# Products that nobody reads, issued in TensorE's waits ahead of the loop over batches

## The chip, the cores and the metric

The kernel runs on one core of a Trainium2 chip. The metric is the device time of one execution in microseconds (us); of several executions the median counts.

## The reference, cut to what matters

The input x has 8 batches of 512 rows of 128 numbers, fp32. One layer of attention with 16 heads of 8 numbers, then a layer norm, then a mixture of 16 experts (8 chosen for each row) and one shared net, then a layer norm.

```python
result = embeddings @ w_qkv                      # [8, 512, 384], split into q, k, v, 16 heads of 8
scores = jnp.einsum('bnqd,bnkd->bnqk', q, k) / jnp.sqrt(jnp.float32(h))
probs = jax.nn.softmax(scores, axis=-1)
ctx = jnp.einsum('bnqk,bnkd->bnqd', probs, v)
x = _layernorm(x + out)                          # out: ctx with its heads side by side
x = _layernorm(x + ffn(x))                       # ffn: the experts and the shared net
```

## The kernel before, in words

Each engine runs its own program in order; semaphores join them. PE is TensorE, DVE is VectorE, ACT is ScalarE, POOL is GpSimd, SP starts most DMAs. First all eight batches go through attention, then all eight through the nets. The 16 heads are 4 groups of 4, the 512 rows 4 tiles of 128: a unit is one group of one batch, with 16 score products (4 heads by 4 tiles).

Scores are made twice. A product of `score_q` (L832, 32 rows of the array, 512 columns, fp32r, a type whose product is one pass) has the queries on the partitions; DVE takes the maximum of each row out of PSUM (`take_maximum`, L776). PE turns a unit's 64 maxima per partition (`turn_maxima`, L882), ACT copies them, DVE or POOL splits them into two parts, and SP writes them to DRAM and loads them into two rows of `q_aug`. Then `score_k` (L839) makes the same scores with the keys on the partitions and the maxima already subtracted, ACT takes the exponential (L733), and `weigh_values` (L852, fp32, several passes) sums the values.

Order on PE: `score_q` runs two units (AHEAD = 2, 32 products) ahead of `score_k`. So there is a **prelude** before the body of batch 0: projections of batch 0 (`project_qk` L886 twice, `project_v` L891), then the wait for the first slot of `q_aug` and `k_aug` to come back from DRAM, then 32 products of `score_q`, with the turning of the first unit's maxima after the 19th. A product of `score_q` waits until DVE is done with the product that had its PSUM bank before; four banks go round. In the body, step i (0 to 63) issues `score_k(i)` and the `score_q` of two units on; after steps 5 and 8 come the projections of the next batch, after steps 11, 14, 20 and so on a `weigh_values`.

In the prelude DVE sets `k_aug` to -1 and `q_aug` to 0 in slot 0 (L811, L812) and reports it on `pads_set`; SP writes these rows to DRAM. ACT stages and rounds the projections (`first_qk`, L715, L716) into `qk_high`, DVE makes `qk_low` (L787), SP writes both to `q_rows` and `k_rows` (L519) and then loads the slots (L508, L511). The PSUM tiles `ps_k1` and `ps_k2` are unused until the body.

Of the kernel before, what the change touches and what calls it, by code (L numbers as in the profile page):

```python
# [28 lines left out]
P = 128  # L29
BATCHES, SEQ, HIDDEN = 8, 512, 128  # L30
# [98 lines left out]
def slot_user_before(i):  # L129

    j = i - 1
    while SCORE_SLOT[j % SCORES] != SCORE_SLOT[i]:
        j -= 1
    return j


def q_head_tile(i):

    return (i + 2) % GROUP, i // GROUP % TILES


def slot_loads(times):

    return DMA * 2 * times
# [285 lines left out]
def attention(nc, r, c, stream, nets_high, nets_low, nets_down, ident, x_tiles, xT, w_qkv,  # L430
              w_nets, w_downs, gate_wT, expert_bias, q_rows, k_rows, shift_rows):
    with ExitStack() as ctx:
        def sb(name, shape, dt=F32):
            return ctx.enter_context(nc.sbuf_tensor(name, shape, dt))

        def psum(name, shape):
            return ctx.enter_context(nc.psum_tensor(name, shape, F32))

        def sem(name):
            return ctx.enter_context(nc.semaphore(name))  # L440


        q_aug = sb("q_aug", [P, GROUPS, SEQ], F32R)
        k_aug = sb("k_aug", [P, GROUPS, SEQ], F32R)
# [3 lines left out]
        w_sb = sb("w_sb", [P, 3 * HIDDEN])  # L448
        qk_raw = sb("qk_raw", [P, 2, SEQ])
        qk_high = sb("qk_high", [P, 2, SEQ], F32R)  # L450
# [9 lines left out]
        ps_k = [psum(f"ps_k{i}", [P, SEQ]) for i in range(3)]  # L460
        ps_ctx = psum("ps_ctx", [P, SEQ])

        def bank(*use):
            return ps_bank[BANK[use]]
# [5 lines left out]
        pads_set = sem("pads_set")  # L470
# [355 lines left out]
        def _(pe):  # L826
            def score_q(i):

                g = i // UNIT
                h, t = q_head_tile(i)  # L830
                rows = slice(h * ROWS, (h + 1) * ROWS)
                return pe.matmul(bank("q", (i - UNIT * AHEAD) % SCORES)[:], q_aug[rows, g, t * P:(t + 1) * P],  # L832
                                 k_aug[rows, g, :], start=True, stop=True).then_inc(scores_q, 1)

            def score_k(i):

                g, t, h = i // UNIT, i // 4 % 4, i % 4
                rows = slice(h * ROWS, (h + 1) * ROWS)
                return pe.matmul(ps_k[SCORE_SLOT[i]][:], k_aug[rows, g, t * P:(t + 1) * P], q_aug[rows, g, :],  # L839
                                 start=True, stop=True).then_inc(scores_k, 1)  # L840
# [15 lines left out]
            def wait_bank(use, b, first=False, last=False, ahead=False):  # L856

                user = bank_user_before(use, first, last, ahead)
                if user is None:
                    return  # L860
                (what, n), ago = user
                b = b - ago
                if what == "q":
                    pe.wait_ge(scores_q_used, SCORES * b + n + UNIT * AHEAD + 1)
                if what == "max":
                    pe.wait_ge(shift_staged, GROUPS * b + n + 2)
                if what == "context":
                    pe.wait_ge(c.ready, 2 * b + n)
                if what == "qk":
                    pe.wait_ge(qk_staged, 2 * (b + 1) + n + 1)  # L870
                if what == "v":
                    pe.wait_ge(v_staged, b + 2)
                if what == "x1":
                    pe.wait_ge(r.x1T_ready, 1)
                if what == "gate":
                    pe.wait_ge(r.decayed, 1)
                if what == "combine":
                    pe.wait_ge(r.combine_copied, 1)

            def turn_maxima(u, parity, dst):  # L880
                pe.wait_ge(scores_q_used, UNIT * (u + 1))
                pe.transpose(dst[0:GROUP * TILES, 0:P], maxima[:, parity, :], ident[:]  # L882
                             ).then_inc(maxima_turned, 1)
# [5 lines left out]
            def project_v(dst):  # L889
                for t in range(TILES):  # L890
                    last = pe.matmul(dst[:, t * P:(t + 1) * P], xT_sb[:, t * P:(t + 1) * P],  # L891
                                     w_sb[:, 2 * HIDDEN:3 * HIDDEN], start=True, stop=True)
                last.then_inc(v_projected, 1)

            def body(b, first=False, last=False):
                for g in range(GROUPS):
                    u = GROUPS * b + g
                    maxima_of_next = not last or g < AHEAD
                    g_next = (g + AHEAD) % GROUPS
                    for i in range(UNIT * g, UNIT * (g + 1)):  # L900
                        if i == UNIT * g:

                            pe.wait_ge(shift_loaded, GROUP * DMA * (u + 1))
                        before = slot_user_before(i)
                        if not first or before >= 0:
                            pe.wait_ge(exp_done, SCORES * b + before + 1)
                        score_k(i)
                        if maxima_of_next:
                            if i == UNIT * g:

                                pe.wait_ge(slot_loaded[g_next], slot_loads(b + 1 + (g + AHEAD) // GROUPS))

                            wait_bank(("q", i), b, first, last)
                            score_q((i + UNIT * AHEAD) % SCORES)
                        if i in QK_AFTER and not last:
                            part = QK_AFTER.index(i)
                            wait_bank(("qk", part), b, first, last)
                            pe.wait_ge(xT_loaded, DMA * (b + 2))
                            project_qk(part, bank("qk", part))
                        if i == V_AFTER and not last:  # L920
                            wait_bank(("v", 0), b, first, last)
                            project_v(bank("v", 0))
                        if i == X1_AFTER and last:
                            wait_bank(("x1", 0), b, first, last)
                            turn_x1(pe, r, ident, bank("x1", 0), 0)
                        if i == CONTEXT_AFTER[0] and not first:
                            wait_bank(("context", 0), b, first, last)
                            turn_context(pe, c, ident, 2 * b - 1, 1, bank("context", 0))
                        if i == CONTEXT_AFTER[1]:
                            wait_bank(("context", 1), b, first, last)  # L930
                            turn_context(pe, c, ident, 2 * b, 0, bank("context", 1))
                        if i == GATE_AFTER and last:
                            wait_bank(("gate", 0), b, first, last)
                            pe.wait_ge(r.consts_loaded, 2 * DMA)
                            gate(pe, r, bank("gate", 0), 0)
                        if i == COMBINE_AFTER and last:
                            wait_bank(("combine", 0), b, first, last)
                            turn_combine(pe, r, ident, bank("combine", 0), 0)
                        if i + SCORES == WEIGH_AFTER[-1] and not first:
                            weigh_values(GROUPS * b - 1, GROUPS - 1, TILES - 1, None)  # L940
                        if i in WEIGH_AFTER:
                            of, t = divmod(WEIGH_AFTER.index(i), TILES)
                            weigh_values(GROUPS * b + of, of, t, None if first and of < PAIR else 2 * b + of // PAIR)
                        if i == MAX_AFTER[g] and not (last and g == GROUPS - 1):
                            wait_bank(("max", g), b, first, last)
                            turn_maxima(u + 1, (g + 1) % 2, bank("max", g))

            pe.wait_ge(xT_loaded, DMA)
            pe.wait_ge(w_loaded, DMA)

            project_qk(0, c.ps_turned)
            project_qk(1, ps_ctx)
            project_v(ps_k[0])
            for u in range(AHEAD):
                pe.wait_ge(slot_loaded[u], slot_loads(1))
                for i in range(UNIT * u, UNIT * (u + 1)):
                    wait_bank(("q", i + UNIT * AHEAD), -1, ahead=True)
                    score_q(i)
                    if i == UNIT + 2:
                        wait_bank(("max", GROUPS - 1), -1, ahead=True)  # L960
                        pe.wait_ge(ident_set, 1)
                        turn_maxima(0, 0, bank("max", GROUPS - 1))
            body(0, first=True)
            with pe.Fori(1, BATCHES - 1) as b:
                body(b)
# [313 lines left out]
```

## Time and profile before

| | |
|---|---|
| median of 3 runs | 733.43 us |
| lowest, highest | 732.75, 737.33 us |
| the profiled execution, its own time | 730.02 us |
| its span, first to last instruction | 728.3 us |
| PE busy in the span | 696.1 us (96%) |
| mean granted clock of TensorE | 0.957 |

The profiled execution took 1.7 us outside its span and was 3.4 us under the median. A granted clock of 1.00 is TensorE's 2.4 GHz, 0.50 is 1.2 GHz. A busy time of PE is modelled from the starts of pipelined products, so the step from one start to the next tells more than the duration of one.

### The profile page before, as it was taken

The page shows a single profiled execution, that of the slowest core. Times are in us where ns is not written, and L with a number is a line of the kernel's source. Part 1 is how long each engine was busy: PE and PEld are TensorE (multiplying, and loading weights), DVE is VectorE, ACT ScalarE, POOL GpSimd, SP SyncE. Part 2 cuts the span into 40 slices and gives each one's busy share as a digit, 9 for nine tenths or more (in the row PEclk, how much of TensorE's full clock was granted, in tenths as well). Part 3 has the DMA queues.
Part 4 walks back from the last instruction along what each step waited for, and adds up shares of the span by engine and source line. Part 5 has one row for each costly group of instructions (what it writes and reads, how often), then busy time and mean ns, then how long its engine had stood idle before and what let it go on. Part 6 is the DMA issues. An engine that isn't in the chain of part 4 may idle for free. (4 is left out here: it accounts for less than half of the span.)

```text
span 728.3 us, 13274 instructions
## 1 busy us (share of the span) xinstructions
PE 696.1 (96%) x3488; PEld 365.0 (50%) x3488; DVE 515.4 (71%) x1085; ACT 415.5 (57%) x779; POOL 321.3 (44%) x371
## 2 busy tenths in 40 slices
PE   2899999999999999999998999999999999999995
PEld 1333333433433343343333767666676767676663
DVE  1879999999999999999851645647555655656343
ACT  2058887988879788887776423333342434324321
POOL 3033342425225242432320665666574656565563
PEclk8559999999999999999897999999999999999998
DMA  6832241423324142241104113050605032140601
GB/s 186 240 119 78 84 155 49 153 68 91 118 81 136 51 139 80 71 154 40 38 5 186 47 73 162 17 230 0 247 0 220 26 127 119 37 209 3 244 1 29
DMA packets 34279, 74.89 MB, mean 103 GB/s; under 512 B 4144, under 2 KB 13488, under 8 KB 30032
## 3 DMA queue, kind: packets, MB, share of 16 engines
q1 hardware_dynamic: 33440, 72.38, 28.7%
q0 software_dynamic: 816, 2.23, 1.1%
q8 instruction: 11, 0.18, 0.1%
q14 instruction: 12, 0.10, 0.0%
HBM read 58.61 MB, written 15.99 MB: 102 GB/s over the span
## 5 line engine op out<-in xcount | busy, mean ns | idle before, releaser
L733 ACT ACTIVATE probs<-ps_k 128x512 f32<-128x512 f32 x512 | 268.2, 606 | 59.4 <-PE ps_k L839 56.1
L776 DVE TENSOR_REDUCE maxima<-ps_bank 128x1 f32<-128x512 f32 x384 | 245.4, 684 | 27.0 <-PE ps_bank L832 21.2
L1061 POOL TENSOR_TENSOR hidden<-gated,weights 128x512 f32<-128x512 f32 x128 | 167.1, 1312 | 124.1 <-DVE gated L1143 108.3
L1091 ACT ACTIVATE silu<-ps_gate 128x512 f32<-128x512 f32 x136 | 81.3, 598 | 176.9 <-PE ps_gate L1185 176.6
L839 PE MATMUL ps_k<-q_aug,k_aug 32*128 32x512 f32 x512 | 161.4, 498 | 3.9 <-ACT probs L733 3.7
L1143 DVE TENSOR_TENSOR gated<-silu,ps_up 128x512 f32<-128x512 f32 x128 | 87.0, 686 | 105.2 <-PE ps_up L1185 69.7
L832 PE MATMUL ps_bank<-k_aug,q_aug 32*128 32x512 f32 x384 | 149.8, 515 | 12.1 <-DMA q_aug<-q_rows 8.2
L852 PE MATMUL ps_ctx<-probs,v_ones 128*32 128x512 f32 x1024 | 142.4, 629 | 0.7 <-ACT probs L733 0.7
L1210 PE MATMUL ps_y<-hidden,nets_down 128*128 128x512 f32 x272 | 137.1, 591 | 0.0
L839 PEld LDWEIGHTS ps_k<-q_aug,k_aug 32*128 32x128 f32 x512 | 66.8, 188 | 131.9 <-ACT probs L733 111.4
L1182 PE MATMUL ps_gate<-x1T_high,nets_low 128*128 128x512 f32 x136 | 96.5, 710 | 0.0
L608 POOL TENSOR_TENSOR shift<-shift_raw,ones 16x128 fp32r<-16x128 f32 x31 | 13.8, 445 | 181.9 <-ACT shift_raw L701 181.9
L776 DVE TENSOR_REDUCE maxima<-ps_turned 128x1 f32<-128x512 f32 x128 | 87.4, 683 | 4.6 <-PE ps_bank L832 3.5
L832 PEld LDWEIGHTS ps_bank<-k_aug,q_aug 32*128 32x128 f32 x384 | 61.7, 192 | 28.1 <-DVE maxima L776 15.8
L832 PE MATMUL ps_turned<-k_aug,q_aug 32*128 32x512 f32 x128 | 65.6, 513 | 1.3
L1210 PEld LDWEIGHTS ps_y<-hidden,nets_down 128*128 128x128 f32 x272 | 51.3, 189 | 15.6 <-issue 3.8
L1185 PE MATMUL ps_gate<-x1T_low,nets_high 128*128 128x512 f32 x136 | 53.6, 394 | 0.0
L1185 PE MATMUL ps_gate<-x1T_high,nets_high 128*128 128x512 f32 x136 | 53.6, 394 | 0.0
L1185 PE MATMUL ps_up<-x1T_low,nets_high 128*128 128x512 f32 x136 | 53.4, 393 | 0.0
L1182 PE MATMUL ps_up<-x1T_high,nets_low 128*128 128x512 f32 x136 | 53.2, 391 | 0.0
L1185 PE MATMUL ps_up<-x1T_high,nets_high 128*128 128x512 f32 x136 | 53.2, 391 | 0.0
L1185 PEld LDWEIGHTS ps_gate<-x1T_high,nets_high 128*128 128x128 f32 x136 | 25.8, 190 | 24.9 <-issue 24.5
(109 smaller groups left out, 631.5 us busy)
## 6 DMA issues: line engine op xcount, KB each, us to landing
weights<-combine_rows SPq DMA_DIRECT2D x32, 1024.0 KB, 7.5
k_aug<-k_rows SPq DMA_DIRECT2D x32, 256.0 KB, 2.6
q_aug<-q_rows SPq DMA_DIRECT2D x32, 256.0 KB, 2.9
q_rows<-qk_high SPq DMA_DIRECT2D x16, 256.0 KB, 2.9
k_rows<-qk_high SPq DMA_DIRECT2D x16, 256.0 KB, 3.6
net_raw<-w_nets POOLq DMA_DIRECT2D x17, 128.0 KB, 2.4
xT_sb<-xT SPq DMA_DIRECT2D x8, 256.0 KB, 2.9
q_rows<-qk_low SPq DMA_DIRECT2D x8, 256.0 KB, 3.1
```

What stands on the lines that cost most here:

```text
L608: pool.tensor_tensor(shift[:, 0, :], shift_raw[:], r.ones[0:GROUP * TILES, 0:P], ALU.mult).then_inc(shift_high, 1)
L733: act.activation(probs[:, t, h, :], ps_k[SCORE_SLOT[i]][:], ACT.Exp, scale=ATT_SCALE).then_inc(exp_done, 1)
L776: dve.tensor_reduce(maxima[:, parity, TILES * h + t:TILES * h + t + 1], bank("q", (i - UNIT * AHEAD) % SCORES)[:], AX_X, ALU.max).then_inc ...
L832: return pe.matmul(bank("q", (i - UNIT * AHEAD) % SCORES)[:], q_aug[rows, g, t * P:(t + 1) * P], k_aug[rows, g, :], start=True, stop=True) ...
L839: return pe.matmul(ps_k[SCORE_SLOT[i]][:], k_aug[rows, g, t * P:(t + 1) * P], q_aug[rows, g, :], start=True, stop=True).then_inc(scores_k, 1)
L852: last = pe.matmul(ps_ctx[32 * h:32 * (h + 1), :], v_ones[:, g, t, h, :], probs[:, t, h, :], start=opens, stop=closes)
L1061: pool.tensor_tensor(hidden[:, s % RING, :], gated[:, s % UP_RING, :], r.weights[:, e, :], ALU.mult).then_inc(hidden_done, 1)
L1091: act.activation(silu[:, s % UP_RING, :], ps_gate[s % 2][:], ACT.Silu).then_inc(silu_done, 1)
L1143: dve.tensor_tensor(dst, silu[:, s % UP_RING, :], ps_up[s % UP_RING][:], ALU.mult).then_inc(gated_done, 1)
L1182: pe.matmul(dst[:], nets_low[:, s, j, :], r.x1T_high[:], start=True, stop=False)
L1185: return pe.matmul(dst[:], nets_high[:, s, j, :], x[:], start=False, stop=stop)
L1210: pe.matmul(ps_y[:], nets_down[:, n, :], hidden[:, n % RING, :], start=n == 0, stop=n == LAST).then_inc(down_done, 1)
```

## The change

It adds products on PE whose results go to `ps_k1` and `ps_k2` and are read by nobody, in four places: 7 products of the constants in slot 0, once DVE has set them and before the wait for the inputs; 9 products of the weights `w_sb` (fp32, 384 columns) between `project_v` and the first `score_q`; one product of `qk_high` (fp32r, 512 columns, all 128 rows) behind each of the 32 products of `score_q`; and 4 of these before the body. One wait is new, for `pads_set`. No other engine's program changes.

```diff
+            def busy_with_pads(dst):
+                pe.matmul(dst[:], k_aug[:, 0, 0:P], q_aug[:, 0, :], start=True, stop=True)
+            def busy_with_weights(dst):
+                pe.matmul(dst[:, 0:3 * HIDDEN], w_sb[:, 0:HIDDEN], w_sb[:], start=True, stop=True)
+            def busy_with_rows(dst):
+                pe.matmul(dst[:], qk_high[:, 0, 0:P], qk_high[:, 1, :], start=True, stop=True)
+            pe.wait_ge(pads_set, 2)
+            for n in range(7):
+                busy_with_pads(ps_k[1 + n % 2])
             pe.wait_ge(xT_loaded, DMA)
             pe.wait_ge(w_loaded, DMA)
             project_qk(0, c.ps_turned)
             project_qk(1, ps_ctx)
             project_v(ps_k[0])
+            for n in range(9):
+                busy_with_weights(ps_k[1 + n % 2])
             for u in range(AHEAD):
                 pe.wait_ge(slot_loaded[u], slot_loads(1))
                 for i in range(UNIT * u, UNIT * (u + 1)):
                     wait_bank(("q", i + UNIT * AHEAD), -1, ahead=True)
                     score_q(i)
+                    busy_with_rows(ps_k[1 + i % 2])
                     if i == UNIT + 2:
                         wait_bank(("max", GROUPS - 1), -1, ahead=True)
                         pe.wait_ge(ident_set, 1)
                         turn_maxima(0, 0, bank("max", GROUPS - 1))
+            for n in range(4):
+                busy_with_rows(ps_k[1 + n % 2])
             body(0, first=True)
```

On PE, from its first instruction to the first scores, before and after (L951, L954 and L957 are the three new helpers in the order of the diff):

```order
 L825 UNCONDITIONAL_BRANCH [waits barrier_Pool_Activation_PE_DVE_SP_release]
+L951 MATMUL ps_k<-q_aug,k_aug 128x512 [waits pads_set]
+L951 MATMUL ps_k<-q_aug,k_aug 128x512 x6
 L886 MATMUL ps_turned<-xT_sb,w_sb 128x512 [waits w_loaded,xT_loaded]
 L886 MATMUL ps_ctx<-xT_sb,w_sb 128x512
 L891 MATMUL ps_k<-w_sb,xT_sb 128x128 x4
+L954 MATMUL ps_k<-w_sb 128x384 x9
 L832 MATMUL ps_bank<-k_aug,q_aug 128x512 [waits slot_loaded0]
+L957 MATMUL ps_k<-qk_high 128x512
 L832 MATMUL ps_turned<-k_aug,q_aug 128x512
+L957 MATMUL ps_k<-qk_high 128x512
 L832 MATMUL ps_bank<-k_aug,q_aug 128x512
```

Nothing is moved; the projections now stand behind seven products and the first score behind nine more.

On PE, around the turning of the first unit's maxima (L882), as it stands now:

```order
L832 MATMUL ps_turned<-k_aug,q_aug 128x512 [waits scores_q_used]
L957 MATMUL ps_k<-qk_high 128x512
L882 MATMUL ps_bank<-ident,maxima 16x128 [waits scores_q_used,ident_set]
L832 MATMUL ps_bank<-k_aug,q_aug 128x512 [waits scores_q_used]
L957 MATMUL ps_k<-qk_high 128x512
L832 MATMUL ps_bank<-k_aug,q_aug 128x512 [waits scores_q_used]
L957 MATMUL ps_k<-qk_high 128x512
```

Each score there has a product of all 128 rows behind it that waits for nothing but PE.

## Rows read from the trace of the kernel before

**Rows 1.** The page: TensorE's granted clock in 40 slices of the span.
```profile
PEclk8559999999999999999897999999999999999998
```

**Rows 2.** Busy time in stretches: start:end, length, busy time of each engine (instructions), granted clock, DMA.
```profile
4.57:10.03 5.46, 5.45 (x12) 3.09 (x12) 1.26 (x2) 2.15 (x4) 0.00 (x0) 1.00 0.37 110
10.03:14.10 4.07, 0.00 (x0) 0.00 (x0) 0.12 (x1) 0.58 (x1) 2.36 (x5) 1.00 0.95 307
...
18.23:37.87 19.64, 16.54 (x34) 7.46 (x34) 17.17 (x30) 0.41 (x2) 0.00 (x0) 0.50 0.86 247
37.87:49.07 11.20, 11.20 (x32) 4.26 (x31) 8.08 (x14) 6.62 (x13) 3.81 (x5) 0.50 0.11 31
...
51.70:84.60 32.90, 32.07 (x229) 11.82 (x223) 31.17 (x54) 27.79 (x56) 10.74 (x19) 1.00 0.30 93
```

**Rows 3.** The timeline of all engines, 1 to 18.3 us: start, duration, instruction.
```profile
1.60 0.48 DVE L812 MEMSET q_aug<- 128x512 f32 x1
...
4.57 2.04 PE L886 MATMUL ps_turned<-xT_sb,w_sb 128*128 128x512 f32 x2 [4.57 <-DMA w_sb<-w_qkv]
...
7.75 1.16 SPq L519 DMA_DIRECT2D q_rows<-qk_high  x2
...
18.23 0.79 PE L832 MATMUL ps_bank<-k_aug,q_aug 32*128 32x512 f32 x1 [8.21 <-DMA q_aug<-q_rows]
```

**Rows 4.** The timeline of PE, from the first unit's turned maxima to step 12 of the body.
```profile
29.50 0.38 PE L882 MATMUL ps_bank<-ident,maxima 128*16 128x128 f32 x1
31.29 1.39 PE L832 MATMUL ps_bank<-k_aug,q_aug 32*128 32x512 f32 x2 [1.42 <-DVE maxima L776]
...
37.87 0.79 PE L839 MATMUL ps_k<-q_aug,k_aug 32*128 32x512 f32 x1
...
42.76 2.08 PE L886 MATMUL ps_turned<-xT_sb,w_sb 128*128 128x512 f32 x2
...
45.91 2.07 PE L886 MATMUL ps_turned<-xT_sb,w_sb 128*128 128x512 f32 x2
...
49.07 1.94 PE L852 MATMUL ps_ctx<-probs,v_ones 128*32 128x512 f32 x8
50.93 0.79 PE L839 MATMUL ps_k<-q_aug,k_aug 32*128 32x512 f32 x1
```

**Rows 5.** The timeline of DVE, the same stretch.
```profile
30.36 0.28 DVE L782 TENSOR_TENSOR shift<-shift_raw,shift 16x128 fp32r<-16x128 f32 x1 [1.63 <-ACT shift L706]
30.57 1.27 DVE L776 TENSOR_REDUCE maxima<-ps_bank 128x1 f32<-128x512 f32 x2
31.76 0.67 DVE L776 TENSOR_REDUCE maxima<-ps_turned 128x1 f32<-128x512 f32 x1
...
40.12 3.65 DVE L776 TENSOR_REDUCE maxima<-ps_bank 128x1 f32<-128x512 f32 x6
45.63 1.89 DVE L776 TENSOR_REDUCE maxima<-ps_bank 128x1 f32<-128x512 f32 x3 [1.85 <-PE ps_bank L832]
48.78 1.89 DVE L776 TENSOR_REDUCE maxima<-ps_bank 128x1 f32<-128x512 f32 x3 [1.27 <-PE ps_bank L832]
51.80 0.69 DVE L776 TENSOR_REDUCE maxima<-ps_turned 128x1 f32<-128x512 f32 x1 [1.13 <-PE ps_bank L832]
```

**Rows 6.** The timeline of PE at the full clock: batch 1, then the nets.
```profile
89.42 0.50 PE L839 MATMUL ps_k<-q_aug,k_aug 32*128 32x512 f32 x1
...
91.48 0.50 PE L839 MATMUL ps_k<-q_aug,k_aug 32*128 32x512 f32 x1
...
92.36 1.06 PE L852 MATMUL ps_ctx<-probs,v_ones 128*32 128x512 f32 x8
93.36 0.50 PE L839 MATMUL ps_k<-q_aug,k_aug 32*128 32x512 f32 x1
...
399.34 0.40 PE L1185 MATMUL ps_up<-x1T_high,nets_high 128*128 128x512 f32 x1
399.57 0.39 PE L1185 MATMUL ps_gate<-x1T_low,nets_high 128*128 128x512 f32 x1
```

## The prediction

> **What bounds the kernel now.** The page's slices and the busy times come first. PE is busy 96% of the span and its clock stands at 1.00 over most of it, at half only at the start and around two short places [rows 1]. So the body of attention and the nets are TensorE's, and time won or lost ahead of the body is carried to the end nearly whole. The prelude is another matter. The stretches [rows 2] show what binds it: nothing runs on PE from 10.03 to 18.23 us, while the rows of batch 0 go to DRAM and come back; from 18.23 to 37.87 DVE is busy 17.17 of 19.64 us and PE merely follows it; then to 49.07 PE is busy all of the time, at the low clock. The timelines of PE and DVE [rows 4, 5] show the order in detail.
>
> The low clock costs something in that last part alone. DVE takes a maximum every 0.60 us (30.57 to 31.76 for two) [rows 5]; a score at either clock is shorter than that, so the 19.64 us owe the clock nothing but a tenth here and there. In steps 5 to 12 of the body DVE stands still three times for PE: 1.85, 1.27 and 1.13 us, 4.25 us in all [rows 5]. Three steps with a projection take 3.15 us there (42.76 to 45.91, and 45.91 to 49.07) [rows 4], 2.06 at the full clock in batch 1 (89.42 to 91.48) [rows 6]. From 51.70 on the clock reads 1.00 [rows 2]. So **4.25 us is about all there is to win** in the body, if the clock were full from its first step.
>
> One row misleads: 4.57 to 10.03 reads 1.00, but two projections there start 1.83 us apart, as the 2.04 of the first at the start and the 2.08 of the same product at 0.50 say too [rows 3, 4]. These ran at 1.2 GHz. The clock rose only with or after them, and 4 us after the last product it was at half again, since the next row reads 0.50 [rows 2].
>
> **The prices.** At the full clock a one-pass product of 512 columns starts 0.23 us after the one before (399.34, 399.57) [rows 6]. At the low one no row of the trace has it alone on all rows of the array. `weigh_values` steps 1.86 us (49.07 to 50.93) [rows 4] against 1.00 (92.36 to 93.36) [rows 6], so the low price is 0.23 x 1.86 = 0.43, between 0.40 (if only what is streamed slows down from an overlapped start) and 0.46 (twice). An fp32 product of 512 columns steps 1.83 at the low clock; of 384 columns that is 1.37, and 0.74 at the full one by the same ratio (0.65 if the steps of the nets' fp32 products held).
>
> **Part by part.**
>
> 1. The seven products of constants start when DVE has set `q_aug`, 1.60 + 0.48 = 2.08 us [rows 3], and take 7 x 0.43 = 3.0: to 5.1. The inputs are there at 4.57. The first projection is late by 0.5 us, and with it the chain of copies and DMAs that ends at 18.23 [rows 3]. I see no cover: SP's first write of rows at 7.75 [rows 3] stands behind that projection's copy, and all later ones behind it on the same queue. If the clock has risen in the middle of the first projection, the 0.5 comes back; bounds 0 and 0.6. I take 0.5: the load lands at 18.7.
>
> 2. Now PE is dense from 2.1 us. Before, some 5.5 us of products preceded the rise; the same here puts it near 7.6, in the second projection. The rest of the projections' 5.46 us then runs at double speed, to about 9.1. Nine products of weights at 0.65 to 0.74 take 5.9 to 6.7: they end at 15.0 to 15.8. **PE then idles for 3 to 3.7 us**, to 18.7. That is the step on which the case turns. Before, the clock fell within the 4.07 us behind the last product [rows 2]. I take it that it falls here as well, some time before or just after the first scores, since the few products of 32 rows that come first are thin.
>
> 3. At the low clock a score and the product behind it cost PE 0.43 + 0.43 = 0.86 us, since the second needs all rows of the array and so neither runs beside the other. DVE wants a score every 0.60. PE becomes the bound of the prelude. The 19 scores up to the turning of the maxima take 19 x 0.86 = 16.3: from 18.7 to 35.0, where L882 stood at 29.50 [rows 4]: +5.5. From there DVE's split and its next maximum come 1.07 later and PE's next score 1.79 later (29.50, 30.57, 31.29) [rows 4, 5], as before: 36.8. Thirteen more pairs, 11.2: 48.0. Four more products, 1.7: 49.7. The body started at 37.87 [rows 4], so it is **late by 11.8 us**. The maxima's way over DRAM is covered now (turned at 35.0, needed at 49.7).
>
> 4. Something is given back in the body. DVE was four maxima behind at its start and PE had to wait for banks: steps 0 to 5 took 4.89 us (37.87 to 42.76) [rows 4]. Now DVE has caught up; the six scores behind a projection took 1.1 us there (45.91 + 2.07 to 49.07) [rows 4], so PE needs 2.2 and a turning of 0.4, and DVE, which has four banks in hand, 3.6 for six maxima. Between the two I take 3.2, which gives 1.7 back. Steps 6 to 11 give back 2 x (3.15 - 2.06) = 2.2 and the step of `weigh_values` 0.86 more, if the clock is full by then, nothing if not. The five products ahead of the body, the projections and scores behind them leave that open.
>
> The sum: 11.8 - 1.7 = +10.1 with the clock still low, +7.0 with it full from step 6. I take the middle, **+8.5**. Behind it the batches are PE's at the full clock, and nothing takes it away again. The profiled execution's 730.0 becomes 738.5; that one was 3.4 under the median, so the median is **741.9**.
>
> **The step that a rule speaks to.** From 37.87 to 49.07 PE is busy 11.20 of 11.20 us and the clock stays at 0.50 [rows 2]; these are mostly products of 32 rows with two dense projections among them. The Trainium skill ("TensorE: Matmul & The Clock Gate", Part 1) says that the default is the throttled clock and that sustained matmul activity releases it. Read as "a busy PE", the rule contradicts this row; and it would free the clock early in the 28 us of back-to-back pairs of step 3. By it the sum would be that of rival B. I weigh the row higher, because a pair there is half a thin product, but a pair is denser than what the row has, so B keeps a good chance.
>
> **Rivals.**
>
> A, the forecast: the clock falls in the wait for the slots and stays low through the pairs. Chance 0.50.
>
> B: it falls but comes back after some 6 us of pairs, as at the start. Seven pairs late by 0.26 each are 1.8; the idle 1.42 us of PE at the turned maxima [rows 4] may drop it once more, another 1.8. With the 0.5 of step 1 and the 4.25 of the body: -1.9 to -0.1, so about 732.4. Chance 0.22. Also here: the clock rises late, the nine products run at the low price (12.3 us from 10.5 to 22.8, late by 4.1), and all is full afterwards: 4.1 + 0.5 - 4.25 = +0.4.
>
> C, the other side: the nine products leave too short a gap, the clock never falls, every pair costs PE 0.46 of DVE's 0.60 and is covered, and the body starts at full clock: 0.5 - 4.25 = -3.8, 729.6. It decides if the idle before the load is short enough; the 3 to 3.7 us against 4.07 that sufficed for a fall are near it. But the 1.4 us at the turned maxima must not drop it either. Chance 0.18.
>
> D: A, and a pair costs more than 0.86 at the low clock because the load of 128 columns of weights for each is not hidden. With 0.1 more per pair, 32 pairs are 3.2 and the four others 0.4: +12.1, 745.5. Chance 0.10.
>
> **How the numbers follow.** The likeliest case is A, 741.9; its own range is 738 to 746. The range of 8 in 10 takes D in and reaches down over B to the edge of C: 729.5 to 745.5. A change of under 1%, 7.3 us, is what a measurement of this kernel can't well tell from none: above 740.8 counts as slower. That holds for D and three fifths or so of A, 0.43 with little of the rest; faster than 726.1 needs more than C has, 0.04; the rest is 0.53.
>
> **What would show it.** Step 1: L886 first at 5.1 instead of 4.57. Step 2: the last weights product near 15 to 16 and a clock of 0.50 in the stretch behind it. Step 3: scores 0.86 apart where they were 0.60, L882 near 35, the first L839 near 50. Step 4: no DVE wait of over 1 us behind step 5 if the clock is back. If the clock reads 1.00 from 19 to 38 us and scores stay 0.60 apart, A is wrong and C holds.

## The result, and the profile after

The changed kernel takes 763.45 us (761.52 to 765.10, 4 runs) against 733.09 (730.90 to 737.33, 4 runs): a ratio of 1.0401, 95% interval 1.0360 to 1.0442. It is 30 us slower. The prediction had forecast 8.5 us and a range that ended at 745.5. The profiled execution took 765.10 us, 1.7 above the median.

The page of the profile after, TensorE's granted clock in 40 slices, answers to [rows 1]:

```profile
PEclk9555899799999999999989899999999999999998
```

Two slices read 5 before; now three do, and a fourth reads 8. Busy times in stretches after (columns as in [rows 2]):

```profile
7.78:13.75 5.97, 5.97 (x20) 3.23 (x18) 0.94 (x2) 0.99 (x3) 2.37 (x5) 1.00 0.85 249
14.00:17.90 3.90, 0.00 (x0) 0.00 (x0) 0.00 (x0) 0.00 (x0) 0.00 (x0) 1.00 0.54 177
18.70:37.87 19.17, 19.17 (x28) 7.67 (x27) 9.44 (x14) 0.00 (x0) 0.00 (x0) 0.50 0.73 214
37.87:67.07 29.20, 27.78 (x42) 11.27 (x42) 12.35 (x19) 0.41 (x2) 0.00 (x0) 0.50 0.09 29
67.07:76.98 9.91, 9.91 (x31) 4.09 (x30) 5.85 (x10) 6.20 (x13) 3.81 (x5) 0.50 0.11 27
76.98:83.40 6.42, 6.42 (x32) 1.79 (x31) 4.17 (x8) 3.54 (x8) 2.16 (x2) 0.50 0.63 208
```

DVE, which was busy 17.17 of 19.64 us in the prelude before [rows 2], is now busy 9.44 of 19.17. PE has become the bound there: all of its time is busy, at the low clock. The timeline of PE after, from its first product to the first `weigh_values` (answers to [rows 3, 4]):

```profile
2.13 3.20 PE L951 MATMUL ps_k<-q_aug,k_aug 128*128 128x512 f32 x7 [2.13 <-DVE q_aug L812]
5.17 1.02 PE L886 MATMUL ps_turned<-xT_sb,w_sb 128*128 128x512 f32 x2
...
7.78 5.97 PE L954 MATMUL ps_k<-w_sb 128*128 128x384 f32 x18
17.93 0.49 PE L832 MATMUL ps_bank<-k_aug,q_aug 32*128 32x512 f32 x1 [4.17 <-DMA q_aug<-q_rows]
...
18.82 0.79 PE L832 MATMUL ps_turned<-k_aug,q_aug 32*128 32x512 f32 x1
19.54 0.79 PE L957 MATMUL ps_k<-qk_high 128*128 128x512 f32 x1
20.26 0.79 PE L832 MATMUL ps_bank<-k_aug,q_aug 32*128 32x512 f32 x1
...
44.72 0.41 PE L882 MATMUL ps_bank<-ident,maxima 128*16 128x128 f32 x1
...
64.64 2.50 PE L957 MATMUL ps_k<-qk_high 128*128 128x512 f32 x5
67.07 0.79 PE L839 MATMUL ps_k<-q_aug,k_aug 32*128 32x512 f32 x1
...
76.98 1.94 PE L852 MATMUL ps_ctx<-probs,v_ones 128*32 128x512 f32 x8
```

The steps to read are those from one start to the next. 19.54 to 20.26 is 0.72, and so is the one before it: **a score and the product behind it take 1.44 us, not the 0.86 of the prediction**. The turned maxima (L882) stand at 44.72 where they were at 29.50 [rows 4], the body starts at 67.07 instead of 37.87. The row with x5 shows what is dear: from the first of the five products of all rows to the score behind the last are 2.43 us, which is four steps of 0.43 and one of 0.72. A step between two products of all rows is 0.43. A step from a score to a product of all rows, or back, is 0.29 more. Below, this is called a change of kind.

What the 0.29 is made of is another question. Each product has its weights loaded into the array first, and that load is about as long (PEld, the queue of weight loads, after; start, duration, then the idle time before it):

```profile
2.13 2.63 PEld L951 LDWEIGHTS ps_k<-q_aug,k_aug 128*128 128x128 f32 x7 [2.13 <-DVE q_aug L812]
...
20.26 0.28 PEld L832 LDWEIGHTS ps_bank<-k_aug,q_aug 32*128 32x128 f32 x1 [0.44 <-issue]
20.98 0.29 PEld L957 LDWEIGHTS ps_k<-qk_high 128*128 128x128 f32 x1 [0.44 <-issue]
```

The seven loads of the constants follow each other without a pause. In the alternation each load starts after an idle 0.44 us, no earlier than its own product is put down, and lasts 0.28 or 0.29, just the extra. But the body of the same profile speaks against a load as the cause. Behind the same pattern of six scores comes once the turning of the maxima, whose load has 16 columns, and once a projection, whose loads have 128 (PE, then PEld):

```profile
67.66 0.62 PE L839 MATMUL ps_k<-q_aug,k_aug 32*128 32x512 f32 x1
68.22 0.38 PE L882 MATMUL ps_turned<-ident,maxima 128*16 128x128 f32 x1
...
73.27 0.62 PE L839 MATMUL ps_k<-q_aug,k_aug 32*128 32x512 f32 x1
73.82 2.08 PE L886 MATMUL ps_turned<-xT_sb,w_sb 128*128 128x512 f32 x2
```

```profile
68.22 0.09 PEld L882 LDWEIGHTS ps_turned<-ident,maxima 128*16 128x16 f32 x1 [0.65 <-issue]
...
73.82 0.50 PEld L886 LDWEIGHTS ps_turned<-xT_sb,w_sb 128*128 128x128 f32 x2 [0.65 <-ACT qk_raw L711]
```

The step is the same, 0.55 to 0.56 us, whether the load is recorded with 0.09 us or, as for 128 columns, with 0.28 to 0.29; and it is 0.56 again to the first `weigh_values` (76.42 to 76.98), whose loads have 32 columns. (The extra is in it: four scores start at 67.07, the last two at 67.66, and 0.59 + 0.56 are two products of 0.43 and 0.29.) So the length of the load does not set the price. What does set it, for instance that the array has to finish one kind of product before it takes the other, no run here separates.

### The profile page after: what moved, and what is told of

It reads as the page before. It is cut to its first block and busy times, and to the rows that moved or that the text cites. A ratio compares the mean times of both kernels' runs of the same rounds, so it can differ in the third digit from the quotient of the medians.

```text
span 763.4 us, 13396 instructions
## 1 busy us (share of the span) xinstructions
PE 737.9 (97%) x3549; PEld 383.0 (50%) x3549; DVE 518.6 (68%) x1085; ACT 415.1 (54%) x779; POOL 321.1 (42%) x371
## 5 line engine op out<-in xcount | busy, mean ns | idle before, releaser
L832 PE MATMUL ps_bank<-k_aug,q_aug 32*128 32x512 f32 x384 | 155.0, 524 | 6.3 <-DMA q_aug<-q_rows 4.2
L852 PE MATMUL ps_ctx<-probs,v_ones 128*32 128x512 f32 x1024 | 146.3, 645 | 0.7 <-ACT probs L733 0.7
L832 PE MATMUL ps_turned<-k_aug,q_aug 32*128 32x512 f32 x128 | 67.2, 525 | 1.0
L852 PEld LDWEIGHTS ps_ctx<-probs,v_ones 128*32 128x32 f32 x1024 | 20.7, 111 | 37.1 <-issue 28.2
```

Source lines behind the costliest of these rows:

```text
L852: last = pe.matmul(ps_ctx[32 * h:32 * (h + 1), :], v_ones[:, g, t, h, :], probs[:, t, h, :], start=opens, stop=closes)
```

## The experiments

All of them start from the changed kernel; "body" is the start of its first `score_k`, 37.87 before and 67.07 after. Each time stands beside the kernel before, run on the same chip.

### Without the products among the scores

```diff
-                    busy_with_rows(ps_k[1 + i % 2])
...
-            for n in range(4):
-                busy_with_rows(ps_k[1 + n % 2])
```

> The seven products of constants and the nine of weights stay; the 32 products of all rows among the scores and the four ahead of the body are gone. Theory 1 (the alternation of a 32-row score with a product of all 128 rows costs PE 0.72 us per product at the low clock, where each alone is 0.43): scores 0.60 apart again, L882 near 29.2, body at 37.6, time of before to within 1 us, 732 to 734. Rival (the first 16 products change the clock's state or the loads for the worse): body later than 40 and a time over 736.

Measured: 733.21 us against 732.92, ratio 1.0014 (0.9989 to 1.0039). The timeline of PE:

```profile
18.93 0.79 PE L832 MATMUL ps_bank<-k_aug,q_aug 32*128 32x512 f32 x1 [3.85 <-DMA q_aug<-q_rows]
...
43.47 2.08 PE L886 MATMUL ps_turned<-xT_sb,w_sb 128*128 128x512 f32 x2
```

The first score is 0.7 us later than before, and so is step 5 of the body (43.47 against 42.76 [rows 4]): with the clock still low there, the first 16 products win nothing and cost about what the late first projection costs (5.29 instead of 4.57). They carry none of the 30 us, as expected.

### The products among the scores alone

```diff
-            pe.wait_ge(pads_set, 2)
-            for n in range(7):
-                busy_with_pads(ps_k[1 + n % 2])
...
-            for n in range(9):
-                busy_with_weights(ps_k[1 + n % 2])
...
-            for n in range(4):
-                busy_with_rows(ps_k[1 + n % 2])
```

> Only the 32 products of all rows among the scores are left; no constants, no weights, no four ahead of the body, no added wait. Theory 1: 31 scores 1.45 apart instead of 0.60, body at 18.2 + 27.5 + 1.8 + 18.8 = 66.3 at the latest, some 28 us late, 759 to 763. Rival (the low clock in the pairs comes from the gap that the weights products leave): no difference, since the clock is low here too; so this run only says how much of the 30 us these 32 products carry.

Measured: 761.10 us against 732.92, ratio 1.0369 (1.0322 to 1.0416). Scores stand 1.44 apart and the body starts at 66.51. Both are as expected, to 0.2 us. The 32 products are the loss: 28.2 us of it. The four ahead of the body, at 0.43 each, would be 1.7 more.

### A longer cover of the wait for the slots

```diff
-            for n in range(9):
+            for n in range(16):
                 busy_with_weights(ps_k[1 + n % 2])
```

> The change with 16 products of weights instead of 9, so that PE has no long wait ahead of the first score. Theory 1, whose price is in the alternation and not in the clock: a pair costs 0.42 + 0.43 = 0.85 at the full clock (the two steps before the clock fell: 17.93, 18.35, and 0.47 across the fall), more than DVE's 0.60; body about 0.25 x 32 = 8 us late plus four products, minus 4 us from a full clock in the body: 736 to 741. Rival 2 (the low clock alone makes the loss, a pair at the full clock is hidden behind DVE): scores 0.60 apart, 728 to 730. If the clock falls in spite of it, near 763.

Measured: 758.21 us against 732.92, ratio 1.0358 (1.0314 to 1.0402). PE went straight from the weights to the scores at the full clock, which this timeline of PE and the stretches below it show:

```profile
21.00 0.50 PE L957 MATMUL ps_k<-qk_high 128*128 128x512 f32 x1
21.43 0.50 PE L832 MATMUL ps_bank<-k_aug,q_aug 32*128 32x512 f32 x1
21.86 0.50 PE L957 MATMUL ps_k<-qk_high 128*128 128x512 f32 x1
```

```profile
19.70:25.20 5.50, 5.50 (x14) 2.38 (x13) 4.12 (x6) 0.00 (x0) 0.00 (x0) 1.00 1.02 305
25.30:60.00 34.70, 33.28 (x48) 13.17 (x47) 15.81 (x24) 0.41 (x2) 0.00 (x0) 0.50 0.30 88
```

Two things follow. At the full clock a pair costs 0.86 (21.00 to 21.86), so it isn't hidden behind DVE's 0.60 even there: rival C of the prediction, which counted 0.46 for a pair, would not have come out even if the clock had held. And the clock fell at 25.2 all the same, with PE busy 5.50 of 5.50 us: the pairs did not hold it up. Neither number of my expectation held (736 to 741, or 763): the six or seven pairs ahead of the fall cost 0.86 instead of 1.44, which saves some 4 us, and all others cost what they did.

### Two products, and short products, behind each score

```diff
                     busy_with_rows(ps_k[1 + i % 2])
+                    busy_with_rows(ps_k[1 + i % 2])
```

> The change with two products of all rows behind each score instead of one. Theory 1a (the extra is paid where PE changes between 32-row and 128-row products, 0.29 us per change at the low clock): a pair grows by one product of 0.43, from 1.45 to 1.88, 32 x 0.43 = 13.8 us on top of the change, 775 to 778. Rival 4 (a product of all rows costs 0.72 wherever it stands among the scores): 32 x 0.72 = 23, over 783.

```diff
+            def busy_with_few(dst):
+                pe.matmul(dst[:, 0:P], qk_high[:, 0, 0:P], qk_high[:, 1, 0:P], start=True, stop=True)
-                    busy_with_rows(ps_k[1 + i % 2])
+                    busy_with_few(ps_k[1 + i % 2])
```

> The change with 128 instead of 512 columns in the 32 products behind the scores. Theory 1a (a fixed 0.29 per change at the low clock): such a product steps 0.11 + 0.29 = 0.40, the pair 1.12, 32 x 0.33 = 10.4 us less than the change, about 752 to 754, still far above before. Rival 5 (what is paid is in proportion to the columns, 0.72 for 512): pair 0.72 + 0.18 = 0.90, body some 10 us late, 742 to 745.

Measured against 732.46: 774.23 with two (ratio 1.0584, 1.0555 to 1.0612), 750.29 with short ones (1.0238, 1.0205 to 1.0271). The timelines of PE, with two and then with short ones:

```profile
24.53 0.79 PE L832 MATMUL ps_bank<-k_aug,q_aug 32*128 32x512 f32 x1
25.25 1.22 PE L957 MATMUL ps_k<-qk_high 128*128 128x512 f32 x2
26.40 0.79 PE L832 MATMUL ps_bank<-k_aug,q_aug 32*128 32x512 f32 x1
```

```profile
24.68 0.79 PE L832 MATMUL ps_turned<-k_aug,q_aug 32*128 32x512 f32 x1
25.40 0.48 PE L957 MATMUL ps_k<-qk_high 128*128 128x128 f32 x1
25.81 0.79 PE L832 MATMUL ps_bank<-k_aug,q_aug 32*128 32x512 f32 x1
```

A second product adds 1.87 - 1.44 = 0.43, not 0.72. A quarter of the columns brings the pair to 1.13 = 0.72 + 0.41, and 0.41 is 0.11 + 0.29 and a hundredth. So the extra is a fixed 0.29 us at each change of kind, at the low clock; a price by product or by columns is refuted. The times are 0.8 and 1.7 us below the ranges expected (775 to 778, 752 to 754), which is not explained here.

### Thin products, which change nothing

```diff
+            def busy_with_group(dst, h):
+                rows = slice(h * ROWS, (h + 1) * ROWS)
+                pe.matmul(dst[:], qk_high[rows, 0, 0:P], qk_high[rows, 1, :], start=True, stop=True)
...
+            group_banks = [ps_k[0], ps_k[1], ps_k[2], ps_ctx]
+            pe.wait_ge(v_staged, 1)
+            pe.wait_ge(qk_highs, 2)
...
-                    busy_with_rows(ps_k[1 + i % 2])
+                    other = (q_head_tile(i)[0] + 2) % GROUP
+                    busy_with_group(group_banks[other], other)
...
-            for n in range(4):
-                busy_with_rows(ps_k[1 + n % 2])
```

> Behind each score a product of 32 rows in another row group than the score's, instead of one of all rows; the four ahead of the body are gone; each row group writes a PSUM bank of its own, for which PE waits on v_staged and qk_highs, long past. Theory 1: both kinds use 32 rows, nothing has to empty the array, scores 0.60 apart, time as of the run without these products. Rival 3 (any product behind a score costs 0.72, by its weights load or its semaphore): scores 1.45 apart, over 758.

Measured: 732.95 us against 732.92, ratio 0.9994 (0.9961 to 1.0026). The timeline of PE:

```profile
23.97 0.79 PE L832 MATMUL ps_turned<-k_aug,q_aug 32*128 32x512 f32 x1
23.98 0.79 PE L958 MATMUL ps_k<-qk_high 32*128 32x512 f32 x1
24.57 0.79 PE L832 MATMUL ps_bank<-k_aug,q_aug 32*128 32x512 f32 x1
```

Score and product start together, in two row groups, and the scores are 0.60 apart as before. The same number of products among the scores as in the change, at the same low clock, costs nothing if they have 32 rows. So it is not the number of instructions: each of these has a load of 128 columns too, and PE waits for two more semaphores here than in the change.

### Fewer changes of kind

```diff
-            for n in range(9):
+            for n in range(14):
                 busy_with_weights(ps_k[1 + n % 2])
...
-                    busy_with_rows(ps_k[1 + i % 2])
+                    if i % 4 == 3:
+                        for n in range(4):
+                            busy_with_rows(ps_k[1 + n % 2])
...
                         turn_maxima(0, 0, bank("max", GROUPS - 1))
-            for n in range(4):
-                busy_with_rows(ps_k[1 + n % 2])
+                        for n in range(4):
+                            busy_with_rows(ps_k[1 + n % 2])
```

> 14 products of weights, so that PE waits under 3 us for the slots; the 32 products of all rows in 8 blocks of four, one behind each fourth score, and four more in the wait behind the turned maxima; none extra ahead of the body. 16 changes between kinds instead of 64. Theory 1a: at the full clock a block and two changes cost 4 x 0.22 + 2 x 0.2 = 1.3 us, covered by the banks that DVE has in hand; the clock stays at 1.00 from about 7 us into the body, which starts near 38; DVE's waits of 4.25 us go: 728.5 to 730.5. If the clock falls on the way: low blocks of 2.3 us, 733 to 740.

Measured: 743.51 us against 732.46, ratio 1.0148 (1.0119 to 1.0177). Both expectations missed it, 728.5 to 730.5 for a held clock and 733 to 740 for a fallen one. The profiled execution is the slowest of the six (746.9). In it the clock fell with the first block (timeline of PE, then of DVE):

```profile
20.78 1.76 PE L957 MATMUL ps_k<-qk_high 128*128 128x512 f32 x4
...
31.80 2.07 PE L957 MATMUL ps_k<-qk_high 128*128 128x512 f32 x4
```

```profile
31.90 1.89 DVE L776 TENSOR_REDUCE maxima<-ps_bank 128x1 f32<-128x512 f32 x3 [1.82 <-PE ps_turned L832]
```

From the start of a block to the score behind it are then 2.0 us, and DVE waits 1.82 for that score. I had counted four maxima in hand for DVE at every block. But the fourth score has to wait for a bank, so DVE has already read the first when it starts, and the three left are done before the block is. With the same 32 products, a quarter of the changes costs about a third of the loss (11 us of 30). It is not a clean ratio, as what a block itself costs PE is in it too.

### Six thin products, full clock

The edit of the run with thin products, with 14 products of weights, four products of all rows behind `turn_maxima` as above, none extra ahead of the body, and this behind each score:

```diff
-                    busy_with_rows(ps_k[1 + i % 2])
+                    for n in range(2 * (GROUP - 1)):
+                        other = (q_head_tile(i)[0] + 1 + n % (GROUP - 1)) % GROUP
+                        busy_with_group(group_banks[other], other)
```

> 14 products of weights; behind each score six products of 32 rows, two in each of the other three row groups, each group with its own PSUM bank; four of all rows in the wait behind the turned maxima; none extra ahead of the body. No change between kinds among the scores. Theory 1a: at the full clock two products per group take 0.43 of DVE's 0.60 us; if such thin products keep the clock up together, the body starts near 38 at full clock, 728.5 to 730.5. If the clock falls in spite of them, each group needs 0.86 per score and the prelude is 32 x 0.26 = 8 us late, 738 to 742. Rival (32 rows never count for the clock, however many groups run): the latter.

Measured: 729.24 us against 732.46, ratio 0.9961 (0.9941 to 0.9980), 12 runs from 725.43 to 732.18. This is faster than both kernels, by a little: 0.4% against the kernel before. The profiled execution is the fastest of the twelve (725.43). Its stretches and its timeline of PE:

```profile
6.50:38.50 32.00, 29.52 (x268) 17.93 (x267) 19.09 (x33) 2.96 (x7) 2.37 (x5) 1.00 0.78 228
...
46.55:347.50 300.95, 295.82 (x1952) 116.47 (x1951) 283.38 (x500) 254.71 (x510) 111.57 (x171) 1.00 0.32 101
```

```profile
42.56 1.12 PE L886 MATMUL ps_turned<-xT_sb,w_sb 128*128 128x512 f32 x2
...
46.55 1.07 PE L852 MATMUL ps_ctx<-probs,v_ones 128*32 128x512 f32 x8
```

The first `weigh_values` comes 2.5 us earlier (49.07 [rows 4]), although the first score came 0.6 later (18.81), and it takes 1.07 instead of 1.94. That is what a clock held from the prelude on gained in the body up to there.

### What carries the thin version

Five instead of seven products of constants:

```diff
-            for n in range(7):
+            for n in range(5):
                 busy_with_pads(ps_k[1 + n % 2])
```

> The version with six thin products behind each score (e7_thin6), with 5 instead of 7 products of constants, so that they end at 2.14 + 5 x 0.43 = 4.3, before the inputs are there at 4.6. If the first projection's start is what the chain of loads hangs on, the first score comes near 18.2 instead of 18.8 and 0.5 us more are gained: about 728.7. If the clock then rises later (at 8 instead of 6.5) or falls in a longer wait for the slots, the gain is lost again or the time is near 738.

Measured: 731.85 us against 733.04, ratio 0.9977 (0.9945 to 1.0009), 12 runs from 725.19 to 734.01; neither of the two times expected. In the profiled execution, one of the slower ones (733.53), the clock was full through the prelude and fell inside the body:

```profile
7.70:41.80 34.10, 31.81 (x278) 18.84 (x277) 22.61 (x39) 4.84 (x12) 3.17 (x7) 1.00 0.73 216
42.00:55.40 13.40, 13.40 (x47) 4.03 (x48) 8.03 (x14) 7.17 (x15) 5.07 (x4) 0.50 0.39 121
```

Its first score came at 18.59, not 18.2. No gain from fewer constants is shown.

The thin products of the version with seven constants, without anything ahead of them:

```diff
-            pe.wait_ge(pads_set, 2)
-            for n in range(7):
-                busy_with_pads(ps_k[1 + n % 2])
...
-            for n in range(14):
-                busy_with_weights(ps_k[1 + n % 2])
```

> The same thin products and the four in the wait behind the turned maxima, without the products of constants and of weights and their wait. If these are needed to bring PE to the scores at the full clock: the clock is at 0.50 at 18.2, two products per row group take 0.86 per score, the prelude is 32 x 0.26 = 8 us late at the most: 736 to 741. If the thin products, four groups busy all of the time at the low clock, raise it by themselves: late by 2 to 3 us and then full, 4 us given back: 730 to 733.

Measured: 732.85 us against 733.04, ratio 0.9987 (0.9966 to 1.0008), inside the second range expected. Its stretches:

```profile
18.90:23.20 4.30, 4.30 (x40) 3.75 (x44) 2.98 (x5) 0.00 (x0) 0.00 (x0) 0.50 1.07 333
23.40:43.70 20.30, 18.78 (x206) 10.37 (x198) 18.82 (x33) 3.55 (x9) 0.89 (x2) 1.00 0.57 166
43.90:50.50 6.60, 6.60 (x20) 2.08 (x24) 3.78 (x8) 3.54 (x8) 3.31 (x3) 0.50 0.23 64
```

Thin products in all four row groups did raise the clock, 4.4 us after the first score. But it fell again at 43.8, in the body, behind a stretch in which scores of two units and a turning are PE's only work; the first projection there ran at the low clock. Both this execution and the one with five constants lost it in that place.

So the last run puts products of all rows there:

```diff
                             turn_maxima(u + 1, (g + 1) % 2, bank("max", g))
+                        if first and i == 2:
+                            for n in range(4):
+                                busy_with_rows(ps_ctx)
```

> The version with six thin products behind each score (e7_thin6), and four products of all rows behind the turned maxima of step 2 of the body of batch 0, where PE has scores of 32 rows alone for 4 us (in the profile with five constants the clock fell there at 41.9). If that stretch is what makes some executions slow: the executions from 731 to 732 of that version disappear, median 727 to 728.5. If the block costs as much as it saves (1.1 us on PE, which then is late for DVE): no difference from 729.2.

Measured: 730.44 us against 732.44, ratio 0.9967 (0.9937 to 0.9998), 12 runs from 726.07 to 734.21. No better than without the block. In its profile the clock held through that place and fell at 67.3 for 3.4 us instead. But it had held through that place without the block too, in the profile of the version with seven constants above, so these two profiles show no effect of the block.

The executions of the three versions with constants and weights differ by 7 to 9 us. In all three the slower ones tend to have the lower mean granted clock: here 0.988 at 726.07 us and 0.974 at 734.21. One block doesn't cure it, and what decides where the clock falls stays open. The intervals of the four versions with six thin products overlap (0.9961, 0.9977, 0.9987 and 0.9967 to the kernel before). So the record doesn't show which of their parts carries the 0.4%, or that the others lack it.

## Why the prediction was wrong

**Right: the path.** Case A is what happened, at another price. PE idled from 13.75 to 17.93, 4.2 us (predicted 3 to 3.7), the clock fell among the first scores, the pairs did not bring it back in 48 us, PE became the bound of the prelude, and the products cost more than the whole body had to give. Rival B, the rule of sustained activity read as a busy PE, lost: PE was busy 19.17 of 19.17 us at 0.50 in the stretch from 18.70.

**Step 1, first projection.** Predicted 0.5 us late and at the low clock. It started at 5.17 (as said, 5.1) but at the full clock, behind the constants alone: step to the next 0.86. ACT's copy of it came at 6.23, where it was 6.65 before, and the first score at 17.93 instead of 18.23. Small: -0.3 for +0.5. This profile is the exception: in the eight other profiles with seven constants the first projection ran wholly or mostly at the low clock, the clock rose between 5.9 and 8.2 us, and the first score came at 18.8 to 19.7 (the latest behind 16 products of weights), nearer to the 18.7 predicted.

**Step 2, weights.** 0.66 a product, 5.97 in all: as predicted (5.9 to 6.7).

**Step 3 is the one that failed: "a score and the product behind it cost PE 0.43 + 0.43 = 0.86 us".** Measured 1.44 to 1.45. The clause behind it, that the second needs all rows and so neither runs beside the other, was right; that each then costs what it costs in a row of its own kind was not. Each change between 32-row and 128-row products costs 0.29 us at the low clock and about 0.21 at the full one (a step of 0.43 there, less the 0.22 of a product among its own kind). By the terms of the sum: the turned maxima at 44.72 are 9.7 later than the 35.0 predicted, and 19 pairs by 0.58 less the 0.8 of the earlier start are 10.2. Thirteen more pairs by 0.58 are 7.5. The body came at 67.07 for 49.7, 17.4 later. Case D came nearest, a pair that costs more than 0.86, but with 0.1 per pair where it is 0.58, and a chance of 0.10; so its 745.5 was too low as well. Its reason, a load of weights that is not hidden, is not shown: the steps in the body above are the same for a short load.

Rows of the kernel before had told it (its timeline of PE, with [rows 4]):

```profile
6.40 1.91 PE L886 MATMUL ps_ctx<-xT_sb,w_sb 128*128 128x512 f32 x2
8.11 1.92 PE L891 MATMUL ps_k<-w_sb,xT_sb 128*128 128x128 f32 x8
...
42.04 0.79 PE L832 MATMUL ps_bank<-k_aug,q_aug 32*128 32x512 f32 x1
...
44.77 0.79 PE L839 MATMUL ps_k<-q_aug,k_aug 32*128 32x512 f32 x1
```

From the score at 42.04 to the projection at 42.76 are 0.72 us, 0.29 over the price of a product. From that projection to the scores behind it at 44.77 are 2.01, and from the one at 6.40 to the next product of all rows 1.71, at the same clock: 0.30 less. I used a step among projections for prices (1.83, the first one, which is itself 0.12 above the second) and did not ask about the steps to and from the scores.

**Step 4, what the body gives back.** Predicted 1.7 in steps 0 to 5, and half of 3.1 later. Steps 0 to 5 took 3.60 us (67.07 to 70.67) instead of 4.89: 1.3 given back. The rest gave nothing. The clock stayed low until 83.5, and the three waits of DVE stand there as before, 1.85, 1.27 and 1.13 us. The first of them:

```profile
73.54 1.89 DVE L776 TENSOR_REDUCE maxima<-ps_bank 128x1 f32<-128x512 f32 x3 [1.85 <-PE ps_bank L832]
```

**The sum.** At the first `weigh_values` the profile is 27.9 us late (76.98 for 49.07), of 30.4 in the medians and 35.1 in the two profiled spans. Over the rest of attention the mean clock was 0.96 after and 0.99 before. I put the 2.5 us between 27.9 and 30.4 down to such low stretches, which differ from execution to execution, and to the second `weigh_values` at the low clock; no run separates them.

**The bounds.** A product had the bounds 0.40 and 0.46, and the upper end of the range was case D's 0.1 per pair more. These bounded the clock's effect on a product among its own kind, not the price of a product in its new place. The rows above would have given 0.29 per change; 64 changes are 18.6 us on top of the 8.5 forecast, an estimate of 760.5 us where 763.45 was measured.

## What to carry to other kernels

Work put into an engine's waits is free only if the engine can take it without changing what it is doing. On TensorE here, a product of all rows among products of 32 rows cost a fixed 0.2 to 0.3 us at each change, twice per inserted product, and the gap beside a score was 0.17 us (DVE's 0.60 less 0.43). Fillers of the neighbours' own shape, in other row groups, cost nothing to measure. One per score left the clock at 0.50; with six per score it held at 1.00 through the prelude in three profiles. And bound a new instruction's price by rows in which it stands beside the same neighbours; its price among its own kind is only a lower bound.

## What the hardware showed that I had not expected

- The fixed price of a change between products of 32 rows and of all rows: 0.29 us at 1.2 GHz and 0.21 at 2.4. Each is about the recorded duration of one load of 128 columns of weights (0.28 to 0.29, and 0.18 to 0.19), but a load of 16 columns, recorded with 0.09, was entered with the same step. The Trainium skill ("TensorE: Matmul & The Clock Gate", Part 3) says that weight loads overlap running products only when the row groups differ. A 32-row score and a 128-row product share a group, and step 0.72; the thin product beside a score is in another group, and starts with it. The trace agrees for both. It does not for products of all rows one behind the other: they share all groups, yet they step 0.43 and their loads are hidden. Part 2 of that page in the Trainium skill names the background weight buffer as a second way for a load to go ahead, which would fit those. No run here tests it.
- A PE that was busy but for 1.4 us kept the low clock for 65 us (18.7 to 83.5), and another lost the full one at 25.2 us while busy 5.50 of 5.50. Thin products in four row groups at once raised it within 4.4 us of the first score; scores alone (0.50 from 18.23 to 37.87 [rows 2]), a score and one thin product together (0.50 from 19.5 to 38.9 in that run), or a score and a product of all rows in turn did not.
- Products of constants, -1 times 0, can raise the clock: in the profile of the changed kernel they were PE's only work before the first projection at 5.17, which ran at the full clock. In the eight other profiles with seven constants the clock rose later, between 5.9 and 8.2 us, with up to three us of projections behind the constants.
